# Attention scores by row-tiled head pairs, with mask and minimum in one VectorE operation

## The reference

```
z   = layernorm(x)
q   = z @ Wq.T + bq                                   # 16 heads of 64
k   = [side @ Wk.T + bk ; ctx @ Wgk.T + bgk]          # 512 keys
v   = [side @ Wv.T + bv ; ctx @ Wgv.T + bgv]
att = q k.T / 8 ;  att[:, :256] = -inf where mask     # only the first 256 keys are masked
x1  = x + softmax(att) v @ Wo.T + bo
out = x1 + fp8-quantised product of layernorm(x1) with the FFN weights, + bias
```

## Time and profile before

| what | value |
|---|---|
| median of 3 runs | 2911.33 us (2909.72 to 2912.35) |
| profiled execution, span from first to last instruction | 2906.8 us, 4.5 us below the median |
| instructions | 68146 |
| PE busy | 2793.8 us (96%), 20352 matmuls |
| DVE busy | 2315.1 us (80%) |
| POOL busy | 2099.0 us (72%) |
| ACT busy | 1982.3 us (68%) |
| DMA | 243 MB, 35.6% of 16 engines; the granted TensorE clock is full from the first batch on |

### The profile page before, as it was taken

The page is one execution under the profiler, slowest core; times in us unless marked ns, Lnnn a source line. Parts: engine busy times, 40 slices in busy tenths (PEclk is TensorE's granted clock), DMA queues, the critical chain, the costliest instruction groups (busy, mean ns, idle before and its releaser), DMA issues.

```text
span 2906.8 us, 68146 instructions
## 1 busy us (share of the span) xinstructions
PE 2793.8 (96%) x20352; PEld 2431.0 (84%) x20352; DVE 2315.1 (80%) x3793; ACT 1982.3 (68%) x4742; POOL 2099.0 (72%) x2504
## 2 busy tenths in 40 slices
PE   5999999999999999999999999999999999999997
PEld 4888888888888888888888888888888888888886
DVE  5888778888778887788887788877888877888776
ACT  4666676766677666767666776667676667766674
POOL 4777777777768777777777687777777776877775
PEclk9999999999999999999999999999999999999998
DMA  5333333333333333333343333333333433333331
GB/s 170 82 77 90 76 86 82 80 79 91 72 90 87 76 90 76 87 83 79 79 92 71 90 87 76 90 77 86 85 79 78 93 69 90 87 76 90 78 82 37
DMA packets 176029, 243.02 MB, mean 84 GB/s; under 512 B 25472, under 2 KB 92544, under 8 KB 176000
## 3 DMA queue, kind: packets, MB, share of 16 engines
q1 hardware_dynamic: 176000, 242.66, 35.6%
HBM read 66.40 MB, written 8.39 MB: 26 GB/s over the span
## 4 chain that ended last, share of the span: by engine, by line
PE 61%; DVE 17%; issue 13%; ACT 7%; DMA 1%; DVEq 1%; POOL 0%; SPq 0%; ACTq 0%; POOLq 0%
PE ps_misc L555 20%; PE ps_o L658 10%; PE ps_pt L645 10%; PE ps_misc L599 8%; PE ps_scores L631 5%; PE ps_scores L632 5%; DVE pt_lo L941 5%; DVE kv_out L912 3%; PE ps_scores L634 2%; ACT probs L786 2%; DVE q_lo L889 2%; DVE scr_b L875 1%; DVE o_t L949 1%; ACT zq_out L751 1%; DVE scr_a L877 1%
## 5 line engine op out<-in xcount | busy, mean ns | idle before, releaser
L481 POOL TENSOR_SCALAR probs<-probs,recips 128x512 f32<-128x512 f32 x1024 | 698.4, 694 | 457.0 <-DVE recips L936 456.8
L795 ACT CAST pt_hi<-ps_pt 128x512 fp32r<-128x512 f32 x1024 | 551.7, 595 | 319.8 <-PE ps_pt L645 314.5
L786 ACT ACTIVATE probs<-ps_scores,neg_max 128x512 f32<-128x512 f32 x1024 | 696.0, 688 | 23.5 <-DVE neg_max L932 11.4
L941 DVE TENSOR_TENSOR pt_lo<-ps_pt,pt_hi 128x512 fp32r<-128x512 f32 x1024 | 655.2, 680 | 53.2 <-ACT pt_hi L795 50.3
L932 DVE TENSOR_REDUCE neg_max<-ps_scores 128x2 f32<-128x1024 f32 x512 | 621.1, 1213 | 9.5 <-PE ps_scores L634 9.5
L658 PE MATMUL ps_o<-pt_hi,v_hl 128*128 128x256 f32 x2048 | 554.6, 302 | 1.0 <-DVE o_t L949 1.0
L645 PE MATMUL ps_pt<-ident,probs 128*128 128x128 f32 x4096 | 531.5, 273 | 1.6 <-DVE pt_lo L941 1.6
L658 PE MATMUL ps_o<-pt_lo,v_hl 128*128 128x256 f32 x2048 | 511.4, 281 | 0.0
L645 PEld LDWEIGHTS ps_pt<-ident,probs 128*128 128x128 f32 x4096 | 464.5, 141 | 8.6 <-POOL probs L481 2.0
L631 PE MATMUL ps_scores<-k_hl,q_hh 128*128 128x512 f32 x1024 | 456.8, 446 | 9.0 <-issue 4.7
L632 PE MATMUL ps_scores<-k_hl,q_lo 128*128 128x512 f32 x1024 | 407.1, 398 | 0.0
(11 more groups left out here) (106 smaller groups left out, 6567.1 us busy)
## 6 DMA issues: line engine op xcount, KB each, us to landing
k_hl<-k_split SPq DMA_DIRECT2D x1024, 128.0 KB, 2.3
mask_sb<-mask_dram SPq DMA_DIRECT2D x128, 256.0 KB, 3.3
q_hh<-q_hh SPq DMA_DIRECT2D x256, 128.0 KB, 2.4
x_sb<-x_dram SPq DMA_DIRECT2D x32, 256.0 KB, 2.8
side_raw<-side_t_dram SPq DMA_DIRECT2D x32, 256.0 KB, 3.6
scr_b<-ctx_t_dram SPq DMA_DIRECT2D x32, 256.0 KB, 2.8
out_dram<-y SPq DMA_DIRECT2D x32, 256.0 KB, 2.1
probs<-wq_t_dram SPq DMA_DIRECT2D x1, 1024.0 KB, 5.1
```

Of the source, the lines that this page charges most:

```text
L481: nc.gpsimd.tensor_scalar(probs[:, h % 2, t, :], probs[:, h % 2, t, :], recips[:, h % 2, t:t + 1], 1.0, ALU.mult, ALU.mult).then_inc(norm_ ...
L786: nc.scalar.activation(probs[:, h % 2, t, :], ps_scores[:, h % 2, t, :], ACT.Exp, bias=neg_max[:, h % 2, t:t + 1], scale=-1.0, accum_out=s ...
L795: nc.scalar.copy(pt_hi[:, h % 2, 2 * k:2 * k + 2, :], ps_pt[:, k, :, :]).then_inc(pthi_done, 1)
L941: V.tensor_tensor(pt_lo[:, h % 2, 2 * k:2 * k + 2, :], ps_pt[:, k, :, :], pt_hi[:, h % 2, 2 * k:2 * k + 2, :].bitcast(F32), ALU.subtract). ...
```

## The change

It has five parts.

1. **Scores by pairs.** Keys and queries of two heads lie one above the other (64 partitions each) as `k_hi`, `k_lo`, `q_hi`, `q_lo`, just as the projection leaves them. `unit(pair, t, g)` makes the scores of both heads for one tile of 128 queries: six matmuls of 64 contraction rows, in turn for the upper and the lower head (e = 0, 1), each head in a PSUM bank of its own. There is one unit in every slot, at the head of the slot; in before the two tiles of one head stood there. `ps_scores` shrinks from four banks to two, and each unit waits until both minima of the unit before are done.
2. **Mask and minimum in one.** `mins` runs one `tensor_tensor_reduce` on DVE for each head of the unit: it reads the scores from PSUM and the mask bytes from SBUF (a row of zeros for the second half of the keys), adds and scales them, writes the result to `probs` in SBUF and keeps the minimum. The mask matmuls go. The reduction of 1024 elements a head becomes two fused operations of 512 elements, each with an accumulator read behind it. ACT's exponential now reads and writes `probs` in SBUF. `mins` now stands ahead of `recip` in DVE's slot.
3. **A ring of four heads** for `probs`, `neg_max`, `sums` and `recips`, where there were two.
4. **Splits.** ACT writes the high part of a key, query or z chunk from PSUM straight to its place (`split_his`), and DVE the low part (`split_los`), two operations of 128x256 for keys and queries and one of 128x512 for z. POOL's key split and all DMAs that placed keys and queries are gone.
5. **Two banks** for `ps_misc`, used in turn, each with its own pair of semaphores. `PLACES` stays; `B_EARLY` goes. The first fills are ordered q, k0, k1, v0, v1, and the values' weights have a landing place of their own, so their load no longer waits.

The core of the diff:

```diff
-    def place_keys(kind, n, kv_through):
-        for part, ready in enumerate((kv_hi_part, kv_ready)):
-            wait_apart(sp, "sp", ready, kv_through)
-            for e in range(2):
-                ...
-                sp.dma_start(k_hl[to, n % 2, 2 * int(kind[1]) + e, :].bitcast(F32),
-                             k_split[own, part, :].bitcast(F32)).then_inc(k_placed, 16)
...
-    mm(dst, q_hh[:, n % 2, i, rows], k_hl[:, n % 2, i, :], start=True, stop=False)
-    mm(dst, q_lo[:, n % 2, i, rows], k_hl[:, n % 2, i, :], start=False, stop=False)
-    m = mask_sb[:, n % 2, (i * QT + t) * S:(i * QT + t + 1) * S].bitcast(FP8E5)
-    last = mm(dst[:, 0:S], mask_weight[:], m, start=False, stop=True)
+def unit(pair, t, g):
+    r, a = pair // 2 % 2, pair % 2
+    rows = slice(t * P, (t + 1) * P)
+    if not (isinstance(g, int) and g + t == 0):
+        pe.wait_ge(min_done, 2 * (g + t))
+    for n, (q, k) in enumerate(((q_hi, k_hi), (q_lo, k_hi), (q_hi, k_lo))):
+        for e in range(2):
+            own = slice(e * DK, (e + 1) * DK)
+            last = mm(ps_scores[:, e, :], q[own, r, a, rows], k[own, r, a, :], start=(n == 0), stop=(n == 2))
+    last.then_inc(scores_done, 1)
...
-    V.tensor_reduce(neg_max[:, h % 2, :], ps_scores[:, h % 2, :, :], AX_X, ALU.min).then_inc(min_done, 1)
+def mins(pair, t, g, free=True):
+    ...
+    for e in range(2):
+        ...
+        V.tensor_tensor_reduce(out=p, in0=s, in1=mask_sb[:, row::MASK_ROWS - row, :], scale=MASK_STEP,
+                               scalar=SCORE_LIMIT, op0=ALU.add, op1=ALU.min,
+                               accum_out=neg_max[:, h % RING, t:t + 1]).then_inc(min_done, 1)
...
+def split_his(kind, n, bank, before):
+    act.wait_ge(misc_full[bank], before + 1)
+    for cols, hi, _, bias in split_parts(kind, n):
+        ...
+            last = nc.scalar.activation(hi, ps_misc[:, bank, cols], ACT.Identity, bias=bias)
+    last.then_inc(hi_done, 1)
...
+def split_los(kind, n, bank, before):
+    wait_apart(dve, "dve", hi_done, before + 1)
+    for cols, hi, lo, bias in split_parts(kind, n):
+        ...
+            last = V.scalar_tensor_tensor(out=lo, in0=src, scalar=bias, in1=hi.bitcast(F32),
+                                          op0=ALU.add, op1=ALU.subtract)
+    last.then_inc(misc_free[bank], 1)
...
-    ps_misc = psum("ps_misc", [P, 512])
+    ps_misc = psum("ps_misc", [P, MISC_BANKS, 512])
```

In exps the exponential is now written in place, and waits for each tile's minimum apart:

```diff
-    act.wait_ge(min_done, g + 1)
-    if free:
-        act.wait_ge(pt_full, 2 * (g - 1))
     for t in range(QT):
-        nc.scalar.activation(probs[:, h % 2, t, :], ps_scores[:, h % 2, t, :], ACT.Exp,
+        act.wait_ge(min_done, 2 * (g - h % 2 + t) + h % 2 + 1)
+        p = probs[:, h % RING, t, :]
+        nc.scalar.activation(p, p, ACT.Exp,
```

More of the change, by code:

```diff
@@ L66 @@
 }
-B_EARLY = (1, 2)
-assert all((h, "B") in PLACES and (h + 1, "A") in PLACES for h in B_EARLY)
-LAST_OWN = 10
 SLOT_ORDER = [(h, place) for h in range(H) for place in "AB"]
-PROLOGUE = [("zt_next", 0), ("q", 0), ("k0", 0), ("v0", 0), ("k1", 0), ("v1", 0)]
+PROLOGUE = [("zt_next", 0), ("q", 0), ("k0", 0), ("k1", 0), ("v0", 0), ("v1", 0)]
 WO = ("wo0_prev", "wo1_prev")
@@ L83, in kept @@
             return False
-        return not (last and (kind == "zt_next" or place[0] > LAST_OWN))
+        own = kind in PREV or group > 0
+        return own or not last
     return {place: PLACES[place] for place in SLOT_ORDER if place in PLACES and kept(place, PLACES[place])}
@@ new lines, in run_chunk @@
+                    elif kind in WO and j == 0:
+                        tile = slice(WO.index(kind) * P, (WO.index(kind) + 1) * P)
+                        for p in range(H // 2):
+                            last = mm(dst, o_t[:, p, tile], wo_sb[:, p, :], start=(p == 0), stop=(p == H // 2 - 1))
+                    elif kind == "xq_prev" and j == 0:
+                        bf = dst.bitcast(BF16)
+                        for t in range(DT):
+                            for q in range(QT):
+                                last = nc.tensor.transpose(bf[:, t * S + q * P:t * S + (q + 1) * P],
+                                                           xq[:, q * D + t * P:q * D + (t + 1) * P], ident_bf[:])
+                    elif kind == "ff_prev":
+                        for t in range(DT):
+                            last = mm(dst, xq_t[:, t, j * P:(j + 1) * P], ffn_q[:, t, :],
@@ L854, in _ @@
             o_los(H * B - 1)
-            for j, kind in enumerate(PREV):
+            for kind in PREV:
                 if kind not in WO:
-                    chunk(kind, 0, TAIL_AT + j, 0, 0, B)
+                    chunk(kind, 0, BANK[kind, 0], tail_before(kind))
         @block.vector
@@ L915, in chunk @@
-            def chunk(kind, n, before, kv_before, b):
+                dve.wait_ge(misc_full[bank], before + 1)
+                if v_before is not None:
+                    dve.wait_ge(v_ready, v_before - 1)
+                half = int(kind[1])
+                bias = v_bias[:, half:half + 1, cols].broadcast_to([P, 2, GW])
+                V.tensor_tensor(v_out[:, V_TURN[kind, n], :].rearrange("p (k c) -> p k c", c=GW),
+                                ps_misc[:, bank, :].rearrange("p (k c) -> p k c", c=GW), bias,
+                                ALU.add).then_inc(misc_free[bank], 1)
@@ L916, in chunk @@
+            def chunk(kind, n, c, place):
+                bank = BANK[kind, n]
                 if kind in V_KINDS:
-                    copy_values(kind, n, before, kv_before)
+                    copy_values(kind, n, bank, c.fills_before(place), c.before(place, V_KINDS))
+                elif kind in SPLIT:
+                    split_los(kind, n, bank, c.before(place, SPLIT))
                 elif kind in WO:
-                    t = WO.index(kind)
-                    dve.wait_ge(misc_full, before + 1)
@@ new lines, in attended @@
+            def attended(kind, before, b):
+                t, bank = WO.index(kind), BANK[kind, 0]
+                dve.wait_ge(misc_full[bank], before + 1)
+                dve.wait_ge(xbo_done, b)
+                if t == 0 and not (isinstance(b, int) and b == 1):
+                    dve.wait_ge(out_stored, 16 * (b - 1))
+                V.tensor_tensor(y[:, t, :], ps_misc[:, bank, 0:D], xbo[:, t, :], ALU.add).then_inc(misc_free[bank], 1)
+                if t == QT - 1:
+                    dve.wait_ge(misc_free[bank], before + 1)
+                    moments(0, y, bn_y, mv_y, b)
@@ L1058, in _ @@
             o_adds(H - 1, H * B - 1)
-            for t, kind in enumerate(WO):
-                chunk(kind, 0, TAIL_AT + t, 0, B)
+            for kind in WO:
+                attended(kind, tail_before(kind), B)
             normalise_y(B)
```

539 lines of the change are left out of this document (226 added, 313 removed).

## The result

The changed kernel takes 2957.75 us (median, 2956.49 to 2959.21) beside 2910.52 us for before on the same chip: ratio 1.0164, 95% interval 1.015 to 1.0179. It is slower by 47 us, where 2852 us and faster was forecast. The profiled execution has a span of 2957.4 us. Medians in this document leave out one execution of key_work_without_wait that took 3675.41 us at a mean granted clock of 0.656, where the others of that kernel had 0.98.

A forecast was written before the change was run, and what follows sets the result against it. PE was taken to bound nine slots of a batch and DVE slots 3 to 9. Terms of -0.1 and -1.5 us a batch, thirty-one times -50, with -9 ahead made -59: 2852 us, range 2740 to 2990.

The forecast's parts named there:

- The stretch: Slots 3 to 9 of a batch, 1493.03 to 1530.33 us, 37.30 us long, where DVE was taken to bound.
- unit, nine slots: PE's scores outside the DVE-bound slots: 0.17 us gained a slot, -1.5 us a batch.
- DVE's work in the stretch: Slots 3 to 9: minimum +1.5, keys' low parts +2.6, queries' low parts -1.4 twice, relief from POOL -0.9.
- DVE's waits in the stretch: Waits for the exponential in odd slots and for ACT's high part in slot 7, together +1.1 us a batch.
- start of the stretch, second bank: Value copy of slot 3 earlier, -1.0; z chunk no longer waiting for a value copy, -0.6 us a batch.
- A new wait ... together +1.1: DVE behind the exponential, some 0.15 us in slots 5 and 9, and behind ACT's high part in slot 7, 0.8.
- The relief from POOL: DVE's SBUF-only operations slowed less beside POOL in slots 3 to 9: a quarter of 3.6 us taken, -0.9.
- The keys: Low parts of four key chunks on DVE in slots 3 to 9, +2.6 us, and slot 7's wait, 0.8.
- PE's unit: Six score matmuls in side-by-side pairs, 0.70 us, plus mode switches of 0.12 each: 0.94 us.
- The rival in which the switch empties the array: PE's mode switch costs up to 0.37 us each; with 0.30 each +50 us, 2961; chance 16%.
- The first score matmul: Before the first batch: it starts at about 34 us in place of 43.01, -9 us once.

The follow-up runs named there:

- key_work_without_wait: no_key_low with two operations that wait for nothing given back to DVE at each of the eight places of a keys chunk; 2891.1 us, ratio 0.9938.
- loop_at_block: The changed kernel with DVE's loop body placed at the start of a 256-instruction block; 2915.12 us, ratio 1.0032 to the kernel before.
- key_wait_without_work: loop_at_block with the keys' low part on DVE cut to 8 of 256 columns, its wait for ACT kept; 2868.41 us, ratio 0.9864.
- keys_by_pool: loop_at_block with the keys' split back on POOL, ACT copying the chunk out and freeing the bank; 2865.71 us, ratio 0.9859.
- no_key_low: loop_at_block without the keys' low part on DVE, third product of high parts twice, ACT freeing the bank; 2820.76 us, ratio 0.9704.
- low_parts_later: loop_at_block with the low parts of z, queries and keys half a slot later in DVE's order; 2941.43 us, ratio 1.0122.

## Why the prediction was wrong

The forecast by its own terms, us a batch. The stretch is the one of the earlier trace rows; the stop is the difference between the changed kernel and loop_at_block.

| term | forecast | measured |
|---|---|---|
| unit, nine slots | -1.5 | -1.9 (PE's busy time outside the stretch: 49.31 in loop_at_block, 51.24 before) |
| DVE's work in the stretch (+1.5 +2.6 -1.4 -1.4 -0.9) | +0.4 | -1.8 (34.92 - 36.68) |
| DVE's waits in the stretch | +1.1 | +3.7 (4.32 - 0.62) |
| start of the stretch, second bank | -1.6 | +0.4 (all that the other rows leave over) |
| stop at the loop's end | none | +1.4 |
| sum | -1.6 | +1.8 (90.48 - 88.75 is 1.73) |

Thirty-one times 1.73 are 54, less 8 ahead of the first batch 46; measured 47.

- **A step was missing: DVE's own program.** No term looked at the loop that grows from 209 to 289 instructions, though the order of instructions showed its length. The stop is 1.4 a batch, some 40 us of the run (loop_at_block). The Trainium skill, Runtime: NRT & Kernel Launch, section Instruction fetch mechanics, says that most engines' buffers hold 512 instructions, refilled in blocks of 256, and that a taken branch to a target outside the current two blocks waits for a DMA. The traces agree where they can: 159 packets of instructions against 16, and 2.67 to 3.19 us a stop; which blocks are held at a turn no trace shows. Without the stop the kernel would still have been no faster than before (2915.12 us), and the stretch takes as long (39.18).
- **"A new wait ... together +1.1" was the step that failed in what was priced.** It counted the exponential and one high part, that of slot 7 (0.8; measured 0.69). It left out those in slots 3 and 5, 0.68 and 1.03, and DVE is idle 0.27 before the reciprocal of each odd slot and 0.50 behind the quantisation: 4.32 us in all in place of 0.62. ACT makes the high part only when PE's chunk is done, DVE stands at the low part by then, and nothing can pass it. key_wait_without_work shows that such waits, with the bank held, are worth at most 48 us.
- **The gain at the start of the stretch and from the second bank (-1.6) isn't in the sum.** From the end of the query chunk of slot 2 on PE to the value copy it is 3.66 us (1504.92 to 1508.58) where it was 4.26: 0.6 less, not 1.0. I take it that a DVE that starts sooner only waits longer for ACT; no run shows that by itself.
- **DVE's work: better than forecast, by wrong terms.** The fused operation costs 0.61 start to start, not 0.69. A pair of low parts costs 0.79, not 0.66. The relief from POOL looks larger than the quarter taken: the operation of L882 with 1589 ns now takes 692 in the mean. But it is not POOL's smaller load that did it. Before, a subtraction of POOL lay under it (the first two lines, from the timelines of DVE and POOL in before); in keys_by_pool, where POOL is busy 70% of the time, it takes 692 as well (the third, from its groups by form):
```profile
1513.84 1.66 DVE L882 SCALAR_TENSOR_TENSOR scr_b<-scr_a 128x512 f32<-128x512 f32 x1
1513.23 1.72 POOL L475 TENSOR_TENSOR v_hl<-kv_out,v_hl 128x512 fp32r<-128x512 f32 x1
```
```profile
L843 DVE SCALAR_TENSOR_TENSOR scr_b<-scr_a 128x512 f32<-128x512 f32 x32 | 22.2, 692 | 1.1
```
And in no_key_low, with POOL busy 54%, another operation of the quantisation (L819) takes 1370 ns where it takes 826 in the changed kernel. So the relief is luck of the order.
- **The keys were priced about right as a sum, and the gain around them was not.** The forecast has 2.6 and 0.8 of the new wait, 3.4 a batch; no_key_low says 3.0. The error was to expect the other terms to outweigh them: without its keys the forecast has -1.6 - 3.4 = -5.0 a batch, and a batch of no_key_low takes 86.36 us (1482.05 to 1568.41, the low part of z), 2.4 less than 88.75. So half of the forecast's gain is missing with no low part of keys on DVE at all. The window of its stretch, and the longest wait of DVE in it:
```profile
1530.29:1567.12 36.83, 34.56 (x275) 30.38 (x274) 33.62 (x75) 24.31 (x60) 23.70 (x31) 1.00 0.09 28
```
```profile
1555.71 1.29 DVE L907 TENSOR_TENSOR pt_lo<-ps_pt,pt_hi 128x512 fp32r<-128x512 f32 x2 [1.04 <-ACT pt_hi L750]
```
The forecast without keys has 37.3 - 3.5 = 33.8 us for it. DVE is busy 33.62 but idle 3.2: the waits were mis-sized apart from the keys, too.
- **The clock was no term at all.** Where PE had 2.95 us of work in 6, it ran the next 3 at 1.2 GHz. In loop_at_block the chunk and the transposes there took 2.47 and 1.42 us where elsewhere they take 1.53 and 0.79: 1.6 us in such a batch. I take it as part of what the lateness costs and no cause of its own: the mean clock is 0.973 there and 0.991 in keys_by_pool, but low_parts_later, at 0.985, is 26 us slower than loop_at_block.
- **PE's unit was right:** 0.90, or 0.99 with the 0.09 at the entry, for 0.94. That is a gain of 0.12 at this place (0.21 + 0.90 in place of 0.12 + 1.11); over nine slots PE's busy time fell by more, 1.9, and what the rest is was not traced. The rival in which the switch empties the array came out at 2961 us, next to the measured time, by a wrong cause: it needed 0.23 or more a switch. The rule of the Trainium skill behind it (TensorEngine Tiling (Array Packing), section Tiling Modes: a change of mode drains TensorE) costs at most the 0.09 and the two 0.1 of the rows here.
- **The first score matmul was right:** 34.96 us for 34, from 43.01.

What stays open: how much of the wait's 48 us is DVE's order and how much the held bank. low_parts_later trades one for the other and shows that both cost. A third bank for `ps_misc` would tell them apart and wasn't tried, though there is room: the changed kernel takes seven banks of 512 numbers (two for scores, two for `ps_pt`, one for `ps_o`, two for `ps_misc`), and the kernel before took eight. Nor does any run show what the second bank or the earlier start gave by itself.

## What to carry to other kernels

Before work is moved onto an engine, count its loop's instructions as well as its microseconds: a loop of 289 instructions on DVE stopped once a turn at one place in the program and not at another, and the packets of the instruction queue show it. A part computed by two engines in sequence (high by one, low by another) costs the second engine its wait in order and holds the buffer until both are done; give it to an engine with slack after a copy that frees the buffer. Where an engine is late already, read what its idle time is waiting for: here it was busy less than before and still the bound.

## What the hardware showed that was not expected

- The stop at a loop's end is 2.67 to 3.19 us on DVE and is put down to whichever semaphore the next operation names, or to issue. It cost 0.2 us a batch in the kernel before, where DVE had waits at that place, and 1.4 in the changed one.
- Matmuls of 64 rows in different halves of the array pair up over at least three instructions of one queue: 0.90 us for alternating order, 0.91 for one half after the other.
- The accumulator read (0.08 us) behind a fused reduction is hidden by the next operation: two such operations start 0.61 us apart.
- The same DVE operation with SBUF sources takes 692 or 1661 ns by what POOL does at that moment, not by how busy POOL is: 692 with POOL busy 51% and 70% of the time, 1661 (the median before) with 72%.
